# A decoder kernel's opening: the first half of the context loaded ahead of x and split ahead of the statistics

## What is computed

```python
x = x + xattn0(layernorm(x), ctx)   # 16 query heads, 8 key/value heads, width 128
x = x + ffn0(layernorm(x))          # gate, up, down, rounded weights
x = x + xattn1(layernorm(x), ctx)   # 16 heads, keys and queries normalised
x = x + ffn1(layernorm(x))          # 16 experts, the best two of each row
```

## Time and profile before

| | us |
|---|---|
| median of three runs | 2208.1 (2207.62 to 2208.65) |
| the profiled execution, whole | 2210.05 |
| its span in the trace | 2208.3 |
| TensorE busy | 2077.2 (94%) |
| VectorE busy | 1569.9 (71%) |
| ScalarE busy | 1255.4 (57%) |
| GpSimd busy | 594.0 (27%) |
| granted TensorE clock, mean | 0.972 |

### The profile page before, as it was taken

How to read it: one execution, slowest core, us unless ns; L and a number is a source line. 1 busy time by engine, 2 the same in 40 slices (tenths; PEclk the granted TensorE clock), 3 DMA queues, 4 the chain that set the end, 5 groups by cost and what they waited for, 6 DMA issues and landing times. The chain is left out here.

```text
span 2208.3 us, 36403 instructions
## 1 busy us (share of the span) xinstructions
PE 2077.2 (94%) x11594; PEld 1790.9 (81%) x11594; DVE 1569.9 (71%) x3702; ACT 1255.4 (57%) x3253; POOL 594.0 (27%) x1492
## 2 busy tenths in 40 slices
PE   5999999999999899998999999999999998589992
PEld 5888988888888678887788888888888887378882
DVE  5777777677779884434677777777777776867775
ACT  4554455445455533324776666676666675567771
POOL 2001001001001122223333444434343333144541
PEclk8999999999999999999999999999999998789996
DMA  7232122121220220002111211111121111278886
GB/s 248 82 99 88 63 84 94 59 89 66 85 82 29 75 74 1 1 1 77 49 58 49 77 48 57 47 57 47 69 74 48 47 40 39 86 262 289 290 276 255
DMA packets 78509, 202.12 MB, mean 92 GB/s; under 512 B 8688, under 2 KB 38408, under 8 KB 66208
## 3 DMA queue, kind: packets, MB, share of 16 engines
q1 hardware_dynamic: 68672, 179.37, 23.3%
q0 software_dynamic: 7520, 16.80, 2.2%
q10 hardware_dynamic: 2176, 4.19, 0.5%
HBM read 179.09 MB, written 29.10 MB: 94 GB/s over the span
## 5 line engine op out<-in xcount | busy, mean ns | idle before, releaser
L731 PE MATMUL bank<-l_wkv_hi,l_ctxT 128*128 128x512 f32 (+1 forms) x768 | 224.2, 363 | 8.0 <-PEq L79 7.1
L1241 DVE TENSOR_TENSOR l_pT_lo<-bank,l_pT_hi 128x512 fp32r<-128x512 f32 x256 | 175.0, 684 | 70.5 <-ACT l_pT_hi L1067 70.5
L1061 ACT ACTIVATE l_probs<-l_scored,l_nbias 128x256 f32<-128x256 f32 x256 | 128.6, 505 | 167.1 <-DVE l_nbias L1314 167.1
L731 PE MATMUL bank<-xnT_hi,l_wq_hi 128*128 128x512 f32 x512 | 209.6, 409 | 0.8 <-DVEq L1547 0.7
L731 PE MATMUL bank<-l_wo_hi,l_oT_hi 128*128 128x512 f32 x512 | 208.4, 407 | 0.7 <-DVE l_oT_lo L1241 0.7
L731 PE MATMUL bank<-xnT_hi,l_wq_lo 128*128 128x512 f32 x512 | 201.2, 393 | 0.0
L731 PE MATMUL bank<-xnT_lo,l_wq_hi 128*128 128x512 f32 x512 | 201.1, 393 | 0.0
L731 PE MATMUL bank<-l_wo_hi,l_oT_lo 128*128 128x512 f32 x512 | 200.6, 392 | 0.0
L731 PE MATMUL bank<-l_wo_lo,l_oT_hi 128*128 128x512 f32 x512 | 200.2, 391 | 0.0
L1067 ACT CAST l_pT_hi<-bank 128x512 fp32r<-128x512 f32 x256 | 151.0, 590 | 67.8 <-PE bank L830 67.8
L1329 DVE TENSOR_SCALAR l_probs<-l_probs,l_rden 128x256 f32<-128x256 f32 x512 | 180.8, 395 | 9.0
(11 more groups left out here) (304 smaller groups left out, 5766.5 us busy)
## 6 DMA issues: line engine op xcount, KB each, us to landing
l_ctxT<-ctx_split SPq DMA_DIRECT2D x63, 1024.0 KB, 4.8
moe_raw_gu<-in_L_ffn_gate_up_proj SPq DMA_DIRECT2D x31, 1024.0 KB, 6.1
moe_raw_dn<-in_L_ffn_down_proj SPq DMA_DIRECT2D x31, 512.0 KB, 5.3
l_raw_a<-in_L_xattn_Wq SPq DMA_DIRECT2D x16, 512.0 KB, 5.8
l_raw_a<-in_L_xattn_Wo SPq DMA_DIRECT2D x16, 512.0 KB, 5.6
x_sb<-in_x SPq DMA_DIRECT2D x4, 1024.0 KB, 9.2
l_v_next<-l_kn SPq DMA_DIRECT2D x16, 256.0 KB, 2.0
l_v_lo<-l_v_next SPq DMA_DIRECT2D x16, 256.0 KB, 2.6
```

Source lines behind the costliest of these rows:

```text
L731: mm = nc.tensor.matmul(out, a[x], b[y], start=(i == 0), stop=(i == n - 1))
L1061: ins = nc.scalar.activation(probs[u % 2][:, t, :], src, ACT.Exp, bias=nbias[:, i:i + 1], scale=scale, accum_out=rsum[:, i:i + 1])
L1241: nc.vector.tensor_tensor(pair[1], src, pair[0].bitcast(F32), ALU.subtract).then_inc(done, 1)
```

## The change

The first context half is issued ahead of x groups 0 and 1, and VectorE's four subtractions of context groups 0 and 1 move from behind its normalisation of tile 0 to the head of its list. Nothing else moves on any engine.

```diff
+            load_c(0)
             load_x(0)
             load_x(1)
-            load_c(0)
             load_c(1)
             ahead.sync(sp)
...
+            for g in range(2):
+                context_low(g)
             for g in range(2):
                 dve.wait_ge(k.x_in[g], 16)
                 for t in range(TG * g, TG * (g + 1)):
                     step(nc.vector.bn_stats(k.ln_stats[:, t, :], k.x_sb[:, t, :]), t == TILES - 1)
...
             for t in DVE_TILES:
                 nc.vector.tensor_scalar(xn[t][:, :], k.x_sb[:, t, :], mv[:, t, 0:1], rstd[:, t:t + 1],
                                         ALU.subtract, ALU.mult).then_inc(dve_normed, 1)
-            for g in range(2):
-                context_low(g)
             for t in range(4):
                 row_low(t)
```

## The result

The changed kernel is slower: a median of 2213.85 us (2212.02 to 2215.15, 13 runs) against 2208.8 of the kernel before, a ratio of 1.0021 with a 95% interval of 1.0013 to 1.0028. That is 4.6 us by the ratio, which compares means and leaves out one of the 13 runs of the kernel before, which took 2633.33; the medians are 5.05 apart. Predicted were 3.9 and 2212.0.

A forecast was written before the change was run, and what follows sets the result against it. The opening's release, set by x's chain through statistics, factors and ScalarE, was taken to shift everything behind it. ScalarE's 3.3 + 0.6 = 3.9 us, added to the 2208.1 median, gave 2212.0 us, range 2209.4 to 2214.6.

The forecast's parts named there:

- The landings: Opening loads: context lands at 6.8 us (6.5 to 7.3), x groups at about 9.9 and 13.0.
- The subtractions and the factors: VectorE, opening: subtractions end at 11.79, statistics at 16.69, normalisation factors at 20.41, 4.3 us later than before.
- What is given back: Opening: VectorE's 2.5 us of subtractions leave the place behind the factors; ScalarE starts normalising 3.3 us later, not 4.3.
- TensorE's pace: Opening, x's first four tiles: 16 transposes at slow pace, 21.04 to 24.68, so ScalarE waits 0.6 us.
- The sum: End of opening: ScalarE 3.3 + 0.6 = 3.9 us late, so the release moves from 30.0 to 33.9.
- the one behind the sum: After the opening's release: everything follows it, so the whole shifts by as much as the release, 3.9 us.
- rival B: Behind the release: clock does not drop, matmuls save 2.5 us, whole only 1.4 later, 2209.5; chance 0.17.
- C: Opening loads: context lands late, delaying subtractions, statistics and factors us for us; at 9.0, +6.1, 2214.2; chance 0.20.
- D: Whole kernel: the change does not do what it says, or gains; chance 0.05.
- The two sides of 4.4: Whole kernel: 4.4 us, about 0.2%, is what measurement can tell; within 0.65, slower 0.32, faster 0.03.
- A: The prediction's own case: opening's release and whole 3.0 to 4.8 us later, about a fifth over 4.4; chance 0.58.

The follow-up runs named there:

- the loads alone: Kernel before with only the new load order, the context half ahead of x groups 0 and 1; median 2212.0 us against 2209.36, ratio 1.0013.
- the run with 84 fills: Changed kernel with 84 unused identity transposes on TensorE between context and x; median 2212.51 us against 2208.84, ratio 1.0015.
- the second: Both kernels run once more, unedited, for second profiles: changed 2213.03 us against 2208.84, ratio 1.0018; before 2207.93, ratio 0.9998.
- a fill at the end: Unused identity transposes from TensorE's last x tile to the release: kernel before with 52, ratio 0.9991; changed kernel with 40, 1.001; before with 64 ahead and 44, 0.9988.
- the subtractions alone: Kernel before with the old load order but the context subtractions at the head of VectorE's list; median 2218.59 us against 2209.36, ratio 1.0043.
- the run with 68 fills: Changed kernel with 68 unused identity transposes on TensorE between context and x; median 2212.31 us against 2208.52.

## Why the prediction was right, and where it was off

*The landings.* Taken 6.8, 9.9 and 13.0; found 6.80, and, in the run of the loads alone, 9.34 and 12.56. The context's was hit; that x landed earlier than taken changed nothing, as the subtractions and not x let the statistics go.

*The subtractions and the factors.* Taken 11.79, 16.69 and 20.41 for their end, the end of the statistics and the factors; found 11.80, 16.55 and 20.26. The factors are 4.2 us later instead of 4.3.

*What is given back.* ScalarE's start at 20.29 is 3.1 later, against the prediction's 3.3. On VectorE the saved 2.5 us turned into a wait for ScalarE, as it had said: 1.82 us idle ahead of the first x subtraction, and three shorter waits of 0.2 to 0.5 after it.

*TensorE's pace.* Taken slow for 16 transposes, 21.04 to 24.68, price 0.6 on ScalarE; found 20.89 to 24.56, and the eight after them slow to the last (1.91). The price on ScalarE was 0.9: 3.1 late at its start and 4.0 late at its weight cast, and its last cast came 0.9 earlier in the run with 84 fills. Of the release it was 0.7 to 0.8. The choice between the recorded 1.00 and the pace was the right one. The Trainium skill, in TensorE: Matmul & The Clock Gate (Part 1, What's actually happening), has the throttled state as the default, and this agrees with every profile here in which TensorE had not yet worked.

*The sum.* 33.9 for the release, found 33.9, with GpSimd and VectorE 0.01 us apart. That it fits to a tenth is partly luck. The start of ScalarE was taken 0.2 too late and the price of the pace 0.3 too low, so its 3.9 came out as 4.0. And the prediction's own ends, 33.5 and 33.35, are only 3.7 behind before's last (29.80), not "about 3.9"; they were found at 33.64 and 33.65, 3.85 behind it.

*Where it was off.* The whole lost 4.6 us by the first ratio and 4.0 by the second, against 3.9; both are within what the runs can tell of it. The median itself came out at 2213.85, 1.85 above the forecast; 0.7 of that is the kernel before, whose median over more runs is 2208.8 and not 2208.1. The step that does not hold as it stands is the one behind the sum, that the timeline after the release is before's, moved. In both pairs of profiles the first attention was longer in the changed kernel, by 0.6 and 1.4 us, because more of it ran at half pace: behind the release 1.0 and 1.3 us more, behind the next stall 0.8 and 2.1 more. In the first pair the clock is at 0.50 from 28.5 to 35.3 us before and from 33.3 to 40.1 in the changed kernel, in the second from 27.7 to 34.5 and from 32.8 to 39.7. It is low equally long, but in the changed kernel less of it falls on TensorE's idleness ahead of the first matmul: 0.8 and 1.2 us instead of 1.8 and 2.5. How long TensorE stands does not by itself decide this: after 5.9 to 6.2 us of standing (four of the experiments) the half-pace stretch was 3.7 to 4.3 us, shorter than after the 5.08 and 5.28 of the changed kernel, but after 7.12 us it was 5.9. Why the clock falls where it does stays open, and with two profiles of each kernel it is not shown that the changed kernel always has the longer stretches. The term that rival B priced at -2.5 had in these profiles the other sign.

*The rivals.* B is out: 0.50 behind the release in every profile without a fill at the end. C did not happen, the context landed at 6.75 to 6.92 in all six profiles with the new order, but its mechanism is shown by the subtractions alone. D is out.

*The two sides of 4.4.* By the first ratio the change is slower by over 0.2%, by the second not quite. The prediction gave 0.65 to within and 0.32 to slower; with a forecast of 3.9 and a line at 4.4, half a us decides it, and the measurements do not. With its own forecast half a us below the line, a fifth of A beyond it was little.

## What to carry to other kernels

Before work is put at the head of an in-order engine's list, look at what stands behind it: here four short subtractions held up the statistics, on which three engines wait, while the time they freed later was idle time, because that engine then waited for another. When two loads exchange places, the question is which of the two starts the longer chain; here x starts a chain of statistics, small steps and normalisation, and the context one of a turn and a cast. And TensorE's idle time between two pieces of work is not always free even if it is off the critical path: after 2.87 us and more between context and x the next piece started at half pace here, and engines behind it waited for that, while after 0.41 or 1.88 us it did not.

## What the runs showed of the hardware

The record of the granted clock said 1.00 from 21 to 26 us in both profiles of the changed kernel while transposes started 0.21 us apart, as they do where the record says 0.50; they went at 0.11 later. In the runs where TensorE had been at full pace before, the record followed (0.50 at 21 us in the run with 68 fills). In such a first stretch, before TensorE has been at full pace, these profiles are to be read by the starts of the instructions and not by the record.

Useless transposes of the identity hold the clock up too: 52 of them held it at 1.00 for 6 us, to the release, and made the first attention 1.2 to 2.2 us shorter (708.3 against 709.5 and 710.5). And an idle time of 2.87 us was enough for the clock to fall at the end of it, while those of 0.41 and 1.88 were not.
